# Index columns copied eight gathers ahead of their gather, in place of four, in a graph attention kernel

## What is computed

```python
xn = _layernorm(x)
q, k, v = (xn @ W.T + b per head, 8 heads of 32)
sim = einsum('hed,hed->eh', q[:, dst], k[:, src]) * scale      # one number per head and edge
p = exp(sim - segment_max(sim, dst)[dst])
attn = p / segment_sum(p, dst)[dst]
agg = segment_sum(attn * v[:, src], dst)
x = x + (agg @ Wo.T + bo) + linear_attention(xn)
x = x + mixture_of_experts(_layernorm(x))                      # 8 experts
```

## Time and profile before

| | us |
|---|---|
| median of 3 runs | 1285.04 |
| lowest, highest | 1282.04, 1286.11 |
| the profiled execution | 1296.26 |
| its span in the profile | 1294.5 |
| of it, first gather of the loop (L888) to the last | 255.7 to 903.2 |
| busy: PE, DVE, ACT, POOL | 976.9, 875.1, 475.0, 655.0 |

### The profile page before, as it was taken

How to read it: one execution, slowest core, us unless ns; L and a number is a source line. 1 busy time by engine, 2 the same in 40 slices (tenths; PEclk the granted TensorE clock), 3 DMA queues, 4 the chain that set the end, 5 groups by cost and what they waited for, 6 DMA issues and landing times. The chain is left out here.

```text
span 1294.5 us, 18792 instructions
## 1 busy us (share of the span) xinstructions
PE 976.9 (75%) x4183; PEld 679.3 (52%) x4184; DVE 875.1 (68%) x1736; ACT 475.0 (37%) x1294; POOL 655.0 (51%) x1037
## 2 busy tenths in 40 slices
PE   0899655677777777778677777776688379999996
PEld 0455342455555554545455454554457346666664
DVE  2678655887888797888888788897775313344433
ACT  2466324533443353334434443443425112211220
POOL 0515273577777677777777777776000022222221
PEclk9999867787778787877888787888796569999998
DMA  4243172167667666766676676666023433233320
GB/s 155 88 104 87 52 205 73 41 182 206 178 176 199 177 186 174 204 187 186 177 204 182 177 195 190 191 184 188 4 75 121 175 100 110 93 116 113 114 94 7
DMA packets 82666, 183.55 MB, mean 142 GB/s; under 512 B 11862, under 2 KB 46476, under 8 KB 82629
## 3 DMA queue, kind: packets, MB, share of 16 engines
q0 software_dynamic: 39488, 126.26, 36.0%
q1 hardware_dynamic: 40297, 54.53, 12.8%
q10 hardware_dynamic: 2844, 2.35, 0.6%
HBM read 166.03 MB, written 20.85 MB: 144 GB/s over the span
## 5 line engine op out<-in xcount | busy, mean ns | idle before, releaser
L888 POOL DMA_INDIRECT slot<-kv_d,idx x408 | 401.0, 983 | 177.1 <-issue 72.6
L1129 PE MATMUL at_pa<-at_pv,at_hot 128*125 128x264 f32 x880 | 292.5, 478 | 121.7 <-DVE agg L1010 110.5
L1129 PEld LDWEIGHTS at_pa<-at_pv,at_hot 128*125 128x125 f32 x880 | 190.0, 233 | 200.4 <-DVE agg L1010 104.8
L1119 PE MATMUL at_pq<-q,at_hotT 125*128 x1320 | 192.0, 309 | 11.5 <-POOL at_sign L874 6.7
L980 DVE TENSOR_TENSOR at_prod<-at_pq,slot 128x1024 f32<-128x1024 f32 x110 | 133.8, 1216 | 66.0 <-DMA slot<-kv_d,idx 55.1
L1119 PEld LDWEIGHTS at_pq<-q,at_hotT 125*128 125x128 bf16 x1320 | 140.3, 110 | 47.6 <-issue 14.6
L996 DVE TENSOR_TENSOR at_pv<-slot,at_pp 128x1056 f32<-128x1056 f32 x110 | 136.8, 1244 | 17.4 <-issue 8.6
L914 ACT ACTIVATE at_habs<-iota_w,nloc_e 128x125 f32<-128x125 f32 x440 | 138.0, 384 | 3.4
L987 DVE TENSOR_REDUCE at_sc<-at_prod 128x32 f32<-128x1024 f32 x110 | 133.4, 1212 | 2.0
L918 ACT ACTIVATE at_hot<-at_habs,one_col 128x500 f32<-128x500 f32 x110 | 78.3, 712 | 131.4 <-PE at_pa L1129 98.5
L1570 POOL DMA_INDIRECT out<-slot,node_s x32 | 32.5, 1015 | 166.9 <-DVE slot L1603 166.9
(11 more groups left out here) (289 smaller groups left out, 1348.1 us busy)
## 6 DMA issues: line engine op xcount, KB each, us to landing
slot<-in_w SPq DMA_DIRECT2D x16, 1024.0 KB
locrow<-loc_d SPq DMA_DIRECT2D x28, 500.0 KB
slot<-kv_d,idx POOLq DMA_INDIRECT x408
kv_d<-vst SPq DMA_DIRECT2D x25, 128.9 KB
base<-in_x SPq DMA_DIRECT2D x5, 625.0 KB
kv_d<-kst SPq DMA_DIRECT2D x25, 125.0 KB
row_d<-base SPq DMA_DIRECT2D x5, 625.0 KB
out<-base SPq DMA_DIRECT2D x5, 625.0 KB
```

Source lines behind the costliest of these rows:

```text
L888: pool.indirect_dma_start(slot[par][:, u, :], None, m.kv_d, bass.IndirectOffsetOnAxis(ap=m.idx[:, par, u:u + 1].bitcast(U32), axis=0)).the ...
L1119: mm = pe.matmul(pq[q % 2][:, u * D:(u + 1) * D], hotT[:, 4 * q + u, :], at(m.q3, wins[u // 2])[:, part, :], start=(part == 0), stop=(part ...
L1129: mm = pe.matmul(pa[p % 2][:, 0:H * VW], hot[:, u % 8, :], pv[:, u % 8, :, :].rearrange("p h c -> p (h c)"), start=(u % 2 == 0), stop=(u % ...
```

## The change

The copy behind gather u of a chunk is now that for gather u + 8, or, in the second half of a chunk, for gather u - 8 of the next chunk. Eight columns are copied ahead of the loop in place of four. The two waits, their values, the gathers and the number of copies are as before.

```diff
                         pool.indirect_dma_start(slot[par][:, u, :], None, m.kv_d,
                                                 ...
-                        if u + 4 < steps:
-                            index(c, par, u + 4)
+                        if u + 8 < steps:
+                            index(c, par, u + 8)
                         elif steps == U:
-                            index(c + 1, 1 - par, u + 4 - U)
-                for u in range(4):
+                            index(c + 1, 1 - par, u + 8 - U)
+                for u in range(8):
                     index(2, 0, u)
```

## The result

The changed kernel takes **1205.9 us** (median of 4 runs, 1204.9 to 1206.5) against 1284.5 us on the same chip (4 runs): a ratio of 0.9389, 95% interval 0.9372 to 0.9406. That is 78.6 us faster. Run again on two other chips it took 1210.4 us (ratio 0.9425, 0.9391 to 0.9460) and 1208.8 us (0.9402, 0.9368 to 0.9436).

The account below looks back on a forecast made before the run. POOL's 24.2 us a chunk, above DVE's 23.0, was taken to bound the attention loop. After the change 23 chunks of 23.2 (533) plus 16 for hiccups make 549 against 588, 39 less: 1247 us, range 1225 to 1285.

Parts of the forecast that it names:

- the forecast's bodies: DVE's bodies in the attention loop: 22.8 us each in the mean, 23.2 a chunk with 0.36 of waits.

Follow-up runs that it names:

- the second profiles of both kernels: The kernel before and the changed kernel, each run again word for word with a profile: 1282.4 us and 1210.4 us.

## What to carry to other kernels

Put the producer of what a wait asks for at least one whole instruction further back than the wait's own place in the queue: on GpSimd a wait that is held until the instruction in front ends costs 0.73 us of dispatch, and one that is met early costs nothing. Before a length is multiplied by 23, take it from a second profile too, and look whether each wait inside it was still waiting for what it names: here 11.1 us in front of L1022 in ten bodies, which only some executions have, made the forecast's bodies too long. A stall of another engine can cost more than its length, since TensorE's clock falls in it: between the second profiles of both kernels the waits at the bodies' starts fell by 51.1 us and the bodies themselves by another 20.3. And look which instruction of another engine the tight one has to clear: here a start 0.15 us later separated a gain of 6% from a loss of 1%, so an edit that adds 0.2 us to GpSimd's loop can undo all of it.

## What the runs showed of the hardware

- A gather on GpSimd that starts 0.03 to 0.07 us behind L974 takes 0.97 us; one that starts 0.09 to 0.37 us behind it ends 1.60 us behind its start (1.51 falling to 1.25 us). At 0.08 us both occur.
- Such a gather also lands late: 6.85 us from its end to the product (611.26 + 1.41 to 619.52) where a short one leaves 4.2 us (604.44 to 608.66). It ends once L974 is over, and so beside the `locrow` transfer that L974 releases. With that transfer cut to 64 columns, and gathers later still, it is 2.7 to 3.6 us in 23 bodies of the waiting kernel. So the transfer is the cause there; in the changed order it was not tried.
- After TensorE had stood idle for 6.3 us its granted clock was 0.50 through the first 11 us of the body; kept at work in the wait by 24 more matmuls, it was 0.86 or more there after all ten waits of 3.3 to 4.4 us (bodies 2 to 26).
- GpSimd's hiccup of 1.57 us in place of 0.15 (1.28 to 1.69 in all twenty profiles) comes at the same two gathers, the second of chunk 9's and of chunk 20's quad 0, with four copies ahead or eight. At the two in quad 2 of chunks 14 and 25 it is 1.4 us or more where the index wait is held and 0.15 to 0.97 where it is not. What it is was not tried.
